# The entry of a second attention: bias poured by TensorE, Q evicted by ScalarE, x2's last piece moved, last down products two tiles behind

## The reference

```
x = x + tanh(g_xattn[0]) * cross_attention0(layernorm(x), ctx)          # 16 heads of width 8
x = x + tanh(g_ffn[0])   * (shared_swiglu + top-1 of 8 experts)(layernorm(x))
x = x + tanh(g_xattn[1]) * cross_attention1(layernorm(x), ctx, bias, mask)
x = x + tanh(g_ffn[1])   * ffn_with_low_rank_experts(layernorm(x))
```

```
scores = einsum('bthd,bshd->bhts', q * SCALING, k)
scores = scores + attn_bias[None]
scores = where(key_padding_mask[:, None, None, :], NEG_INF, scores)
attn   = softmax(scores)
```

## Time and profile before

| | us |
|---|---|
| median of three runs | 167.54 |
| the profiled execution | 167.28 |
| its span | 165.5 |
| PE busy | 149.2 (90%) |
| DVE busy | 119.1 (72%) |
| ACT busy | 84.4 (51%) |
| POOL busy | 81.3 (49%) |

### The profile page before, as it was taken

How to read it: one execution, slowest core, us unless ns; L and a number is a source line. 1 busy time by engine, 2 the same in 40 slices (tenths; PEclk the granted TensorE clock), 3 DMA queues, 4 the chain that set the end, 5 groups by cost and what they waited for, 6 DMA issues and landing times.

```text
span 165.5 us, 4223 instructions
## 1 busy us (share of the span) xinstructions
PE 149.2 (90%) x1568; PEld 100.6 (61%) x1568; DVE 119.1 (72%) x328; ACT 84.4 (51%) x184; POOL 81.3 (49%) x99
## 2 busy tenths in 40 slices
PE   7789889998998979999998998877999989989993
PEld 2155558686854467899995433335677666534792
DVE  0599986997578791876773096996899975787551
ACT  3269978878355521444440234148778695552110
POOL 7286964881448776056767223574966631010000
PEclk9999999999999999999999999999999999999999
DMA  4999999997101115644300130000000000000012
GB/s 143 298 426 401 289 261 239 257 202 166 26 0 37 51 49 113 132 77 89 73 12 14 34 97 0 0 2 4 0 4 2 4 0 4 0 0 0 18 48 65
DMA packets 19702, 15.04 MB, mean 91 GB/s; under 512 B 3509, under 2 KB 18231, under 8 KB 19426
## 3 DMA queue, kind: packets, MB, share of 16 engines
q1 hardware_dynamic: 18370, 13.17, 32.1%
q0 software_dynamic: 736, 1.07, 2.1%
q10 hardware_dynamic: 576, 0.53, 1.0%
HBM read 7.78 MB, written 6.91 MB: 89 GB/s over the span
## 4 chain that ended last, share of the span: by engine, by line
PE 56%; DVE 20%; ACT 12%; issue 5%; DMA 3%; POOL 1%; SPq 0%; ACTq 0%; POOLq 0%; DVEq 0%
PE pair L1001 24%; PE bank L1001 23%; PE bank L1085 4%; ACT big L552 3%; DMA xr<-x_in 3%; ACT xn L472 3%; ACT Pe L547 2%; DVE Sa L716 2%; DVE Sa L739 2%; DVE st L674 2%; PE bank L1051 2%; PE bank L1111 1%; DVE xr L971 1%; DVE Sx L901 1%; DVE mx L718 1%
## 5 line engine op out<-in xcount | busy, mean ns | idle before, releaser
L348 POOL TENSOR_TENSOR Sx<-Sa,mx 128x512 f32<-128x512 f32 x22 | 23.0, 1046 | 15.7 <-ACT Pe L547 6.7
L322 POOL TENSOR_TENSOR rstd<-ve,nhalf 128x2 f32<-128x2 f32 x16 | 11.6, 724 | 29.7 <-DVE ve L680 29.5
L547 ACT ACTIVATE Pe<-Sx 128x512 f32<-128x512 f32 x32 | 19.7, 631 | 5.3 <-POOL Sx L348 4.8
L552 ACT ACTIVATE big<-bank 128x512 f32<-128x512 f32 x32 | 18.0, 595 | 6.3 <-PE bank L1085 6.1
L430 POOL DMA_INDIRECT routed_rows<-big x15 | 14.7, 979 | 13.0 <-DVE big L962 8.0
L1085 PE MATMUL bank<-cst,Pe 128*128 128x128 f32 x128 | 18.4, 279 | 1.4 <-ACT Pe L547 1.2
L1085 PEld LDWEIGHTS bank<-cst,Pe 128*128 128x128 f32 x128 | 14.0, 141 | 7.1 <-ACT Pe L547 3.7
L1001 PE MATMUL bank<-Vx,big 128*64 128x18 f32 x448 | 15.6, 212 | 2.0 <-ACT big L552 2.0
L1001 PEld LDWEIGHTS bank<-Vx,big 128*64 128x64 f32 x448 | 14.2, 138 | 5.0 <-ACT big L552 5.0
L1001 PE MATMUL pair<-Kx,QT 32*64 32x256 f32 x256 | 12.9, 399 | 1.9 <-DVE Sa L739 1.4
L472 ACT ACTIVATE xn<-xr,nmr,rstd 128x128 f32<-128x128 f32 x22 | 9.9, 487 | 6.3 <-DVE nmr L686 6.1
(11 more groups left out here) (160 smaller groups left out, 311.2 us busy)
## 6 DMA issues: line engine op xcount, KB each, us to landing
sorted_rows<-empty SPq DMA_DIRECT2D x1, 4752.0 KB, 29.4
wgu<-rgu SPq DMA_DIRECT2D x1, 2048.0 KB, 10.7
wdn<-rdn SPq DMA_DIRECT2D x1, 1024.0 KB, 14.3
big<-sorted_rows SPq DMA_DIRECT2D x15, 66.0 KB, 2.0
ctxT<-ctx_in SPq DMA_DIRECT2D x2, 256.0 KB, 4.4
xr<-x_in SPq DMA_DIRECT2D x2, 256.0 KB, 5.0
wf<-ffn SPq DMA_DIRECT2D x1, 512.0 KB, 5.9
Kx<-KT SPq DMA_DIRECT2D x16, 32.0 KB
```

Source lines behind the costliest of these rows:

```text
L322: pool.tensor_tensor(rstd[:, w], ve[:, w], nhalf[:, w], ALU.pow).then_inc(s_pow, 1)
L348: pool.tensor_tensor(Sx[:, hh, :].rearrange("p (h k) -> p h k", h=HH), Sa[:, (2, n % 2)[hh], :].rearrange("p (h k) -> p h k", h=HH), last_ ...
L547: act.activation(Pe[:, u % 3, :], Sx[:, hh, :], ACT.Exp).then_inc(s_exp, 1)
L552: act.activation(PT[:, 4 * hh:4 * hh + 4, cols(n, P)], bank3(T_BANK[hh], 4), ACT.Copy).then_inc(s_pt, 1)
```

## The change

There are five parts, all about the stretch from the experts' last tiles to the first pairs of the second attention.

1. Pair 0's bias and mask are put into PSUM by PE, by four products of the unit matrix with `bm` of 256 columns in float32 (`pour_bias`), before Q is there. The scores of pair 0 are then added on top. So pair 0 goes the way of the first attention: maximum and subtraction by DVE straight from PSUM for the even half, a copy by ACT (`score_evac`) for the odd half. The constant is `POURED = 1`; the counts of the semaphores are adjusted for it.
2. Q of pieces 0 and 1 leaves PSUM by ACT instead of DVE. The bias, multiplied by the scale, is computed once ahead of the experts' loop (`bqs`).
3. The last piece of x2 (`residual2(3)`) stands before the attention in DVE's program, instead of behind pair 0, and its inverse deviation stands with the others on POOL.
4. PE: 2 products of zeros instead of 4 before the first V projection; the transposition of piece 1 follows the scores of pair 0; the transpositions of pieces 2 and 3 follow the scores of pair 3, and their Q product follows the transpositions of that step; 3 products of zeros instead of 10 in pair 0. ACT copies half of V out before it waits for the scatters, and copies pieces 2 and 3 out behind `pt_evac` of pair 1's odd half.
5. The experts' loop has one step less: the down product of tile 12 is issued in the step of tile 14, ahead of tile 14's gate and up products, and the two after it follow one step earlier. DVE copies tile 12 out ahead of tile 14's gated product.

The core of the diff:

```diff
@@ vector engine: unit_e and max_o
-                if layer == 0:
+                if layer == 0 or n < POURED:
                     link(dve.tensor_reduce(m, heads[0], AX.X, ALU.max))
-                    if n >= 1:
-                        dve.wait_ge(s_exp, 2 * n - 1)
+                    if layer + n >= 1:
+                        dve.wait_ge(s_exp, UNITS * layer + 2 * n - 1)
                     dve.tensor_tensor(Sx[:, 0, :].rearrange("p (h k) -> p h k", h=HH), heads[0],
                                       last_bcast(m, S), ALU.subtract).then_inc(s_sube, 1)
...
-                if layer == 0:
-                    dve.wait_ge(s_ev, evac_count(0, n))
+                if layer == 0 or n < POURED:
+                    dve.wait_ge(s_ev, evac_count(layer, n))
@@ vector engine: x2 and the attention
-                    if n == 0:
-                        q_evac(layer, 1)
-                        if layer == 0:
-                            stats(0, 3)
-                            dve.wait_ge(s_tg, 1)
-                        else:
-                            residual2(3)
+                    if n == 0 and layer == 0:
+                        q_evac(0, 1)
+                        stats(0, 3)
+                        dve.wait_ge(s_tg, 1)
...
-            q_evac(1, 0)
+            residual2(3)
@@ vector engine: the experts' loop
+            def routed_rows(w):
+                dve.wait_ge(s_y, w + 1)
+                dve.tensor_copy(ys[:, w, :], bank[6 + w % 2][:, 0:D]).then_inc(s_ys, 1)
+
             for j in range(SLOT_TILES + 2):
+                if j == SLOT_TILES - 1:
+                    routed_rows(j - 2)
...
-                if j >= 2:
-                    w = j - 2
-                    dve.wait_ge(s_y, w + 1)
-                    dve.tensor_copy(ys[:, w, :], bank[6 + w % 2][:, 0:D]).then_inc(s_ys, 1)
+                if j >= 2 and j != SLOT_TILES - 1:
+                    routed_rows(j - 2)
@@ scalar engine
+            def q_evac(a):
+
+                act.wait_ge(s_bqs, 1)
+                act.wait_ge(s_qp, PIECES + a + 1)
+                act.activation(QT[:, cols(a, TPP * P)], bank[Q_BANK[1][a]][:, 0:TPP * P], ACT.Identity,
+                               bias=bqs[:, 0:1], scale=SCALE).then_inc(s_qt, 1)
...
-                    if n == 2:
-                        xnT_evac_half(2 * layer, 1)
+                    if n == 2 and layer == 0:
+                        xnT_evac_half(0, 1)
...
+                    if n == 0 and layer == 1:
+                        q_evac(1)
...
+                    if n == 2 and layer == 1:
+                        xnT_evac_half(2, 1)
...
-            act.wait_ge(d_yscat, 16 * SLOT_TILES)
-            act.dma_start(yg[:, 1, :], y_dram[P:2 * P, :]).then_inc(d_yg[0], 16)
             for c in range(CH):
                 for e in range(2):
                     v_evac(1, c, e)
+                if c == 0:
+                    act.wait_ge(d_yscat, 16 * SLOT_TILES)
+                    act.dma_start(yg[:, 1, :], y_dram[P:2 * P, :]).then_inc(d_yg[0], 16)
             for a in (0, 1):
                 normalise(2, a)
+                if a == 1:
+                    act.wait_ge(s_rh, SLOT_TILES)
+                    for n in range(POURED):
+                        score_evac(1, n)
                 xnT_evac(2, a)
+                if a == 0:
+                    q_evac(0)
@@ tensor engine
+            def pour_bias(n, hh):
+
+                for g in range(2):
+                    o = pair[hh][:, 256 * (g + 1):256 * (g + 2)].rearrange("p (h k) -> p h k", h=HG)
+                    mm(o, ident, mid_bcast(bm[:, n, :], HG), last=False, skip_group_check=True)
...
+                fresh = layer == 0 or n >= POURED
...
                         ins = mm(o.rearrange("p (h k) -> p h k", h=HG), QT[w, b * S:(b + 1) * S],
-                                 Kx[w, :, b * S:(b + 1) * S])
+                                 Kx[w, :, b * S:(b + 1) * S], first=fresh, skip_group_check=not fresh)
...
+                    if n == 2 and layer == 1:
+                        xn_transpose(2, 2)
+                        xn_transpose(2, 3)
...
                     if n == 0 and layer == 1:
-                        keep_warm(AV_BANK[0], 10)
+                        keep_warm(AV_BANK[0], 3)
...
+                if 3 <= j < SLOT_TILES:
+                    routed_down(j - 3)
+                if j >= SLOT_TILES - 1:
+                    routed_down(j - 2)
 
             pe.wait_ge(s_shr, CH)
+            keep_warm(5, 2)
             for c in range(CH):
+                v_proj(1, c)
                 keep_warm(5, 4)
-                v_proj(1, c)
-            keep_warm(5, 4)
...
             pe.wait_ge(s_ys, SLOT_TILES)
-            keep_warm(6, 12)
+            keep_warm(6, 8)
+            pe.wait_ge(s_ve, 2 * CH)
+            for n in range(POURED):
+                for hh in range(2):
+                    pour_bias(n, hh)
+            keep_warm(6, 4)
```

More of the change, by code:

```diff
@@ L214, in build @@
         ACT_HEADS = 2
+        POURED = 1
         RES_X2, RES_L1 = PIECES, 2 * PIECES
@@ L344, in subtract @@
                 N = PAIRS * layer + n
-                pool.wait_ge((s_mxe, s_mxo)[hh], n + 1 if hh == 0 else evac_count(layer, n))
+                pool.wait_ge((s_mxe, s_mxo)[hh], n + 1 - POURED if hh == 0 else evac_count(layer, n))
                 if N:
@@ L433, in _ @@
                                         bounds_check=T - 1, oob_is_err=False).then_inc(d_yscat, 16)
-            for a in range(PIECES - 1):
+            for a in range(PIECES):
                 rstd_of(2, a)
@@ L634, in _ @@
             attention(0)
+            act.wait_ge(d_att1, 16)
+            act.activation(bqs[:, :], wat[1][:, BQ:BQ + 1], ACT.Copy, scale=SCALE).then_inc(s_bqs, 1)
             for j in range(SLOT_TILES + 1):
@@ L1153, in attention @@
                         transposes(layer, n, 0)
+                    if n == 2 and layer == 1:
+                        q_proj(1, 2, 2)
                     if n == 0 and layer == 0:
@@ L1163, in attention @@
                         values(layer, n - 1)
-                    if n == 1:
-                        xn_transpose(2 * layer, 2)
-                        xn_transpose(2 * layer, 3)
+                    if n == 1 and layer == 0:
+                        xn_transpose(0, 2)
+                        xn_transpose(0, 3)
                     if n >= 2 and n % TPP == 0:
@@ L1307, in _, with routed_down @@
             keep_warm(2, 3)
-            for j in range(SLOT_TILES + 3):
+            def routed_down(w):
+                pe.wait_ge(s_rh, w + 1)
+                if w >= 2:
+                    pe.wait_ge(s_ys, w - 1)
+                for f in range(2):
+                    o = w * 2 * D + f * D
+                    wt = wdn[:, o:o + D] if w < E else wdn[:, bass.ds(first_col[w - E] + f * D, D)]
+                    ins = mm(bank[6 + w % 2][:, 0:D], hrT[:, w % 3, f * P:(f + 1) * P], wt, first=(f == 0), last=(f == 1))
+                ins.then_inc(s_y, 1)
+            for j in range(SLOT_TILES + 2):
                 if j < SLOT_TILES:
@@ L1324, in _ @@
                     ins.then_inc(s_gu, 1)
-                if j >= 3:
-                    w = j - 3
-                    pe.wait_ge(s_rh, w + 1)
-                    if w >= 2:
-                        pe.wait_ge(s_ys, w - 1)
-                    for f in range(2):
-                        o = w * 2 * D + f * D
-                        wt = wdn[:, o:o + D] if w < E else wdn[:, bass.ds(first_col[w - E] + f * D, D)]
-                        ins = mm(bank[6 + w % 2][:, 0:D], hrT[:, w % 3, f * P:(f + 1) * P], wt, first=(f == 0), last=(f == 1))
-                    ins.then_inc(s_y, 1)
+                if 3 <= j < SLOT_TILES:
+                    routed_down(j - 3)
+                if j >= SLOT_TILES - 1:
+                    routed_down(j - 2)
             pe.wait_ge(s_shr, CH)
+            keep_warm(5, 2)
             for c in range(CH):
+                v_proj(1, c)
                 keep_warm(5, 4)
-                v_proj(1, c)
-            keep_warm(5, 4)
             pe.wait_ge(d_lora, 32)
```

38 lines of the change are left out of this document (21 added, 17 removed).

## The result

| | before | after |
|---|---|---|
| median, us | 167.49 (20 runs) | 166.3 (20 runs) |
| the profiled execution, us | 167.28 | 165.97 |
| its span, us | 165.5 | 164.1 |
| PE, DVE, ACT, POOL busy, us | 149.2, 119.1, 84.4, 81.3 | 148.8, 116.8, 85.7, 80.3 |

The ratio of the times is 0.9922, with a 95% interval of 0.9897 to 0.9946: the changed kernel is 0.8% faster, 1.3 us. The forecast was 165.6 us with a range of 164.6 to 166.9. Some executions are slower, at a lower granted clock: every ratio in this document is taken from the others alone, while a median is that of all executions (without the slower ones the kernel before has 167.3, 173.4 and 172.9 us beside the experiments on the first, second and third chip).

A forecast was written before the change was run, and what follows sets the result against it. DVE's own work was taken to bound the way to pair 1's first sum. Terms -0.38 +1.76 -0.80 -0.27 -2.76 -1.22 +2.21 -0.56 make -2.0, cut to -1.8: 165.5 us profiled, 165.6 median, range 164.6 to 166.9.

The forecast's parts named there:

- the zeros in pair 0: PE in pair 0: going from 10 to 3 products of zeros was said to give nothing by itself.
- rival of the late Q: ACT's copy of pieces 2 and 3 slips, DVE stands 1.0 us longer, gain only 0.8: 166.7 us; chance 0.18.
- the 0.2 that it took off for hand-overs: Allowance for some ten hand-overs in a new order, each perhaps a few hundredths longer; gain cut from 2.0 to 1.8.
- The loop's end: Experts' loop: down product moved ahead of tile 14's products, two zeros fewer; low-rank products 0.38 us earlier.
- The poured bias: PE ahead of x2's transposition: four pours at 0.44 us, 1.76 in all, make that transposition 0.58 later than 99.97.
- rival of nearly free pours: Pours cost 0.2 us or less each, so PE is at x2's transposition in time: gain 2.7, 164.6 us; chance 0.12.
- the slower one: Pours keep PE from x2: at 1.10 us each the kernel gets slower, 168.1 us; chance 0.06.
- To pair 1: From x2's transposition through pair 0's scores to pair 1's first sum on DVE: 105.72 instead of 108.17, 2.45 us earlier.
- The piece in the pause: DVE before pair 0: x2's last piece, 1.93 us of DVE before, ends by 103.4, hidden in a pause.
- The last Q is late next: DVE before the last Q's eviction stands 2.3 us for ACT's copy and PE's product; eviction only 1.46 earlier.
- The rule on the shared ports: Two-input SBUF operations of DVE and POOL share ports, loser waits; x2's piece up to 0.6 us later, sum unchanged.

The follow-up runs named there:

- experiments 1 and 2: Changed kernel without the poured bias: 165.32 us, ratio 0.9871; changed kernel with seven zeros fewer ahead of x2's first transposition: 165.73 us, ratio 0.9907.
- experiment 3: Kernel before with only the last piece of x2 moved ahead of the attention (its inverse deviation on POOL): 166.8 us, ratio 0.9967.
- Experiment 6: Changed kernel with pieces 2 and 3 of x2 normalised and transposed earlier: 164.13 us, ratio 0.9801.
- Experiments 4 and 5: Kernel before with x2's last piece moved and 3 zeros in pair 0: 172.83 us, ratio 0.9898; changed kernel with 10 zeros there: 174.03 us, ratio 1.0046.
- experiment 9: Changed kernel with the old loop end: 172.5 us, ratio 0.9961, on the second chip; run again on the third, 171.93 us, ratio 0.9943.
- experiment 7: Changed kernel with pieces 2 and 3 normalised early and seven zeros fewer ahead of x2's transposition: 169.29 us, ratio 0.9749; repeat 168.1 us, ratio 0.9743.

## Why the prediction was right, and where it was off

The mechanisms were right and in the right order, with one exception that entered no term of the sum (the zeros in pair 0, below). The forecast of 165.6 is 0.7 us too low, because nearly every size on the way was taken a little too small, and all in the same direction: pair 4 gained 1.07 us where the sum had 2.02. The time alone would not have told the forecast from its rival of the late Q, for 166.3 is nearer to that rival's 166.7; the trace tells them apart. All places are counted from tile 13's products, and "predicted" is the prediction's time less 84.08, without the 0.2 that it took off for hand-overs at the end.

| step | before | predicted | measured |
|---|---|---|---|
| low-rank products | 9.87 | 9.49 | 9.72 |
| x2's first transposition | 15.89 | 16.47 | 17.01 |
| pair 1's sum | 24.09 | 21.64 | 22.48 |
| pair 3's sum | 31.26 | 27.59 | 28.39 |
| last Q evicted | 32.64 | 31.18 | 32.14 |
| pair 4's sum | 35.69 | 33.67 | 34.62 |

The missing 0.95 at pair 4 is made up of 0.23 at the loop's end, 0.31 at the poured bias, 0.30 in three hand-overs up to pair 1 and 0.14 in two more around the last Q, less 0.03 elsewhere.

- *The loop's end* was the worst sized term for its size: -0.38 predicted, -0.15 measured. The count put a down product's turn of 0.45 in front of tile 14's products and had the last product stay within 0.05. In the trace the two down products side by side take 1.03 (84.65 to 85.68) instead of 0.90, and the last one starts 0.14 behind DVE's gated product, which is itself 0.59 later: 4.45 against 4.17 after tile 13. Without the two zeros taken away the new end would be a loss of 0.28 on this chip.
- *The poured bias* is the row that the trace of before did not have. 0.48 against 0.44 each: 0.16 in all, and the nineteen zeros took 4.31 instead of 4.17, since a run of zeros costs a little more than its number times the pitch inside a long one: eight take 1.83 (94.53 to 96.36) instead of 1.74, and the eleven 2.48 instead of 2.39. So x2's transposition was 0.31 later, counted from the low-rank products, than predicted. The rival of nearly free pours fell with it, and so did the slower one: both needed a price that the measured one is far from. That PE would be late there, and by how much of slack, was read rightly; experiments 1 and 2 show that this lateness costs 1.0 to 1.3 us at pair 4. The prediction did not set the pour against the same kernel without it, and so did not see that the pour loses more here than it saves.
- *To pair 1.* From the transposition to pair 0's maximum 3.05 instead of 2.88: ACT's Q comes 0.80 behind the start of its product (0.73 counted) and the scores 0.62 behind ACT's start (0.53 counted). From there to pair 1's sum 2.42 instead of 2.29: ACT takes the odd half 0.86 behind the scores' start (0.73 counted, which is DVE's hand-over). The 0.2 taken off for all the hand-overs was too little, for these three make 0.3 by pair 1, and the two around the last Q make another 0.14: its product starts 0.73 behind the start of ACT's copy (0.66 counted), and DVE 1.21 behind the product (1.14 counted).
- *The piece in the pause* was right: 1.49 us of DVE gone from the path, and experiment 3 gives 1.80 at pair 1 for it alone.
- *The last Q is late next* was right in place and size: a wait of 2.35 where 2.3 was predicted, for the copy that stands behind `pt_evac`. Both ends of the wait are late by nearly the same, because pair 1's sum is 0.84 late. Experiment 6 removes it and gives 2.20 back. The rival that this wait takes the whole gain had the right place, but needed another microsecond.
- *The zeros in pair 0* was the one sentence that was wrong in kind: "of the zeros the seven that went in pair 0 gave nothing by themselves". It was read from the time at which PE would come to pair 0's transpositions with three; with ten it would have come 1.52 later, at 107.78, more than two microseconds after the end of the exponential that starts near 104.9 and takes 0.63, and I did not work that out. Experiments 4 and 5 put the seven at 1.11 and 1.38 us. Of the 1.81 that piece and zeros bring together in experiment 4, the piece alone brings 0.70.
- *The rule on the shared ports* had an instance in each direction before, and has two more against it now: DVE's addition with two inputs in SBUF takes 0.48 from 100.66, while POOL's power runs beside it:

```profile
98.79 0.79 POOL L324 TENSOR_TENSOR rstd<-ve,nhalf 128x2 f32<-128x2 f32 x1 [0.50 <-DVE ve L702]
100.51 0.79 POOL L324 TENSOR_TENSOR rstd<-ve,nhalf 128x2 f32<-128x2 f32 x1 [0.93 <-DVE ve L702]
```

The Trainium skill, in "SBUF — State Buffer", section "SBUF: two separate sides", would have the later of the two wait for the whole of the other. The piece's addition did not, and neither did the one at 98.95. For this small operation of POOL the trace does not bear the rule out. POOL's own operation was a little longer beside the addition: 0.79, and 0.69 at 102.23, where DVE stands idle.

## What to carry to other kernels

Filler work ahead of a wait is free only as long as the wait is there: whoever puts real work into such a stretch, or makes what it waits for earlier, has to take out as much filler, place by place, and has to work out the time with the old filler too. When a stall on one engine goes, follow the copy that another engine issues in a fixed order behind its own work; here the last Q hung on ACT's order, and an earlier place for two normalisations and their transpositions brought more than the whole change.

## What the runs showed that I had not expected

The same program differs by 3 to 4% between chips. The difference lies in the experts' loop and V's products: the low-rank products start between 93.5 and 94.2 us in all six traces of the first chip, and between 98.2 and 101.5 in the eight of the others. Most of it is waits. In the profile with ten zeros the granted clock is 1.00 all through, single instructions have their usual length, and the low-rank products still start at 98.47. In three of the eight the clock also falls for a part of this stretch: it is 0.83 between 90 and 100 us in experiment 9's first run and in the repeat of experiment 7, where the first V products take 1.98 us instead of 1.15, and 0.89 between 80 and 90 us in experiment 9's second. One of the waits, ACT's copy of tile 13's products, in the changed kernel on the first chip:

```profile
84.85 0.38 ACT L662 ACTIVATE Sa<-pair 128x256 f32<-128x256 f32 x1 [0.62 <-PE pair L1024]
```

and with ten zeros on the third:

```profile
88.91 0.38 ACT L662 ACTIVATE Sa<-pair 128x256 f32<-128x256 f32 x1 [1.18 <-PE pair L1024]
```

It comes 1.10 behind the start of the products in the first (83.75) and 2.21 in the second (86.70), though the two kernels are the same up to there. In the stretch of the table, behind the low-rank products, nothing of it is left. What holds the loop up on those chips is open.
